# Gathers of the attention pass and the gated pass: each lot of four waits for the landing of the lot before

## The reference

```python
h_prime = (x @ W + b).reshape(n, K, F_OUT)
e = leaky_relu(h_src[src] + h_trg[trg]); e = e - max(e)
exp_e = exp(e)
alpha = exp_e / (segment_sum(exp_e, trg)[trg] + 1e-10)
out = segment_sum(h_prime[src] * alpha[:, :, None], trg)
```

```python
ei = concatenate([x[src], edge_attr], axis=-1)
core = maximum(ei @ W1 + b1, 0.0) @ W2 + b2
gate = sigmoid(ei @ Wg + bg)
agg = segment_sum(gate * core, dst)
```

## Time and profile before

| | |
|---|---|
| median of the runs shown | 4390.39 us |
| span of the profiled execution | 5143.9 us |
| busy: TensorE, its weight loads | 3848.2 us (75%), 2836.3 us (55%) |
| busy: VectorE, ScalarE, GpSimd | 2174.4 (42%), 1234.4 (24%), 1935.0 us (38%) |
| mean granted TensorE clock | 0.828 |
| gathers of the attention pass (line 865, 416) | 401.7 us busy, 386.7 us idle before them |
| gathers of the summation pass (line 865, 416) | 393.9 us busy, 211.3 us idle before them |
| gathers of the gated pass (line 865, 416) | 393.5 us busy, 563.7 us idle before them |

### The profile page before, as it was taken

The page is one execution under the profiler, slowest core; times in us unless marked ns, Lnnn a source line. Parts: engine busy times, 40 slices in busy tenths (PEclk is TensorE's granted clock), DMA queues, the critical chain, the costliest instruction groups (busy, mean ns, idle before and its releaser), DMA issues. The chain is left out here.

```text
span 5143.9 us, 62246 instructions
## 1 busy us (share of the span) xinstructions
PE 3848.2 (75%) x19117; PEld 2836.3 (55%) x19117; DVE 2174.4 (42%) x6089; ACT 1234.4 (24%) x3514; POOL 1935.0 (38%) x2021
## 2 busy tenths in 40 slices
PE   3877777234735555458399999996969999999597
PEld 2555555112425444357366665654538887777586
DVE  5555556600344444242300000005237777777723
ACT  3555454200100000012200000001125554444332
POOL 3455453474266666445400000001224444444053
PEclk8778888566866766668699999997579999999598
DMA  6655553000023333036454444443434444444266
GB/s 213 175 148 141 150 152 107 1 19 1 3 83 91 92 89 91 25 112 184 143 153 142 142 136 141 140 133 99 113 126 137 134 137 135 133 130 129 69 218 208
DMA packets 424073, 613.62 MB, mean 119 GB/s; under 512 B 149273, under 2 KB 287650, under 8 KB 423490
## 3 DMA queue, kind: packets, MB, share of 16 engines
q1 hardware_dynamic: 310578, 327.46, 22.2%
q0 software_dynamic: 104112, 273.76, 18.6%
q10 hardware_dynamic: 9056, 8.43, 0.5%
HBM read 517.83 MB, written 91.59 MB: 118 GB/s over the span
## 5 line engine op out<-in xcount | busy, mean ns | idle before, releaser
L2217 POOL DMA_INDIRECT stage<-t_row,f_take x168 | 162.1, 965 | 1269.7 <-POOLq L2064 1152.3
L865 POOL DMA_INDIRECT eg_rows<-t_edge,src_i x416 | 393.5, 946 | 563.7 <-DVE eg_pre L1698 422.1
L1108 PE MATMUL ps<-sum_hot,sum_rows 128*128 128x128 f32 x1664 | 330.0, 364 | 365.6 <-issue 201.5
L1372 PE MATMUL ps<-cv_cells,xn 128*128 128x384 f32 (+2 forms) x1600 | 535.7, 493 | 67.2 <-DMA cv_cells<-t_cells 67.2
L271 POOL DMA_INDIRECT t_cells<-times_seen,cell x416 | 409.8, 985 | 413.0 <-PEq L312 152.8
L865 POOL DMA_INDIRECT ag_rows<-t_att,src_i x416 | 401.7, 966 | 386.7 <-DVE ag_msg L970 264.6
L1108 PEld LDWEIGHTS ps<-sum_hot,sum_rows 128*128 128x128 f32 x1664 | 292.7, 264 | 403.0 <-issue 392.9
L865 POOL DMA_INDIRECT sum_rows<-t_row,src_i x416 | 393.9, 947 | 211.3 <-issue 116.5
L1050 PE MATMUL ps<-featT,ag_msg 128*128 128x128 f32 x1664 | 370.7, 357 | 127.2 <-issue 124.4
L1372 PEld LDWEIGHTS ps<-cv_cells,xn 128*128 128x128 f32 x1600 | 304.2, 190 | 279.5 <-DMA cv_cells<-t_cells 67.6
L1650 PE MATMUL ps<-eg_w,eg_rT 128*128 128x256 f32 x1664 | 439.3, 386 | 1.1 <-ACT eg_rT L1668 1.1
(11 more groups left out here) (418 smaller groups left out, 6296.4 us busy)
## 6 DMA issues: line engine op xcount, KB each, us to landing
cv_cells<-t_cells SPq DMA_DIRECT2D x225, 384.0 KB
cv_cells<-t_cells SPq DMA_DIRECT2D x75, 448.0 KB
xn<-in_L_ffn_W SPq DMA_DIRECT2D x57, 512.0 KB
t_cells<-zeros SPq DMA_DIRECT2D x17, 1664.0 KB
xn<-in_L_ffn_expert_w SPq DMA_DIRECT2D x110, 256.0 KB
ag_trow<-t_dst SPq DMA_DIRECT2D x104, 256.0 KB
t_cells<-zeros POOLq DMA_DIRECT2D x8, 1664.0 KB
eg_eaT<-in_edge_attr SPq DMA_DIRECT2D x208, 64.0 KB
```

The costliest lines, as they stand in the source:

```text
L865: nc.gpsimd.indirect_dma_start(out=rows[:, j, :], out_offset=None, in_=table, in_offset=bass.IndirectOffsetOnAxis(ap=src_i[:, n:n + 1], ax ...
L1108: mm = nc.tensor.matmul(ps[:, j % BANKS, k * EC:(k + 1) * EC], lhs, hot[:, j, :], start=True, stop=True)
L1372: mm = nc.tensor.matmul(ps[:, bank(q, k, half), 0:at.stop - at.start], source(l)[:, s, k * 128:(k + 1) * 128], cells[:, n % CR, at], start ...
L2217: nc.gpsimd.indirect_dma_start(out=xd[:, j, :], out_offset=None, in_=t_row, in_offset=bass.IndirectOffsetOnAxis(ap=take_row[:, n:n + 1], a ...
```

## The change

`gathers` gets a parameter `landed`. Where it is set, GpSimd waits ahead of each lot but the first until all four gathers of the preceding lot have landed, by the semaphores of their slots. It is set in the attention pass and in the gated pass, and not in the summation pass.

```diff
-    def gathers(pool, table, rows, ring, free, beside=None):
+    def gathers(pool, table, rows, ring, free, beside=None, landed=False):
 
         for n in range(NCH):
             j = n % ring
             if n >= ring and n % ER == 0:
                 pool.wait_ge(free.sem, free.at(n - ring + ER))
+            if landed and n > 0 and n % ER == 0:
+                for k in range(n - ER, n):
+                    pool.wait_ge(gath[k % ring].sem, gath[k % ring].at(16 * (k // ring + 1)))
             nc.gpsimd.indirect_dma_start(out=rows[:, j, :], out_offset=None, in_=table,
...
-                    gathers(pool, t_att, rows, R, g.msg_done)
+                    gathers(pool, t_att, rows, R, g.msg_done, landed=True)
...
-                    gathers(pool, t_edge, rows, GE, g.gpre_done, beside=offset)
+                    gathers(pool, t_edge, rows, GE, g.gpre_done, beside=offset, landed=True)
```

## The result

| | median, us | range |
|---|---|---|
| before | 4390.77 | 4388.14 to 4394.56 |
| changed kernel | 4773.99 | 4765.45 to 4804.88 |

The ratio is 1.0884, 95% interval 1.0853 to 1.0915: 383 us slower. Forecast were +160 (4550) and a range that ended at 4620. The direction was right, the size less than half of what came.

A forecast was written before the change was run, and what follows sets the result against it. GpSimd's issue was taken to bound the attention pass at 5.0 to 5.4 us a lot, closely followed by TensorE. Attention +160 (between +142 and +183) and gated 0 gave 4390.39 + 160 = 4550 us, range 4385 to 4620.

The forecast's parts named there:

- A lot then costs 3 x 1.25 + 2.93: Attention pass: three gather issues plus the last one's landing, 6.68 us a lot, 6.78 with the semaphores.
- The 2.93: Attention pass: us from the last gather's issue to VectorE's release, read at the opening.
- restart (four semaphores): Attention pass: four more semaphore instructions a lot, put at 0.1 us, bounds 0 and 0.30.
- The upper bound of the landing, 3.81: Attention pass: a 256 KB load of target numbers at the opening took 3.81 us; lot 7.56, +264 us.
- the gated pass's "0 us": Gated pass: new waits are met before GpSimd's existing wait for VectorE, TensorE being the bound, so no cost.
- The cover of 1.5 us: Gated pass: with a 3.81 us landing the new waits are met 1.5 us before the old wait for VectorE.
- the 753.5 us: Whole kernel: profiled span of 5143.9 us over the 4390.39 median, 17%, read as the recorder holding TensorE back.
- a span near 5072: Profiled execution: shorter rows of gathers end the stalls, attention lot from 7.48 to about 6.8 us, -72 us.
- rival A: TensorE's delays behind long gather rows are the chip's, so timed runs get faster: 72 us at most, 4328; chance 0.12.
- B: Attention pass held by something else, such as SP's loads, at 6.5 to 6.8 us a lot: no difference, 4390; chance 0.11.
- C: Attention pass: the 0.30 us between gathers is the recorder's, lot 5.8 us, +93, 4483; chance 0.20.
- The case that was left out: Attention pass: TensorE, pausing more, gets half its clock and bounds the lot at 8.2 us, some +330.

The follow-up runs named there:

- e4_sum: Kernel before with the landing wait in the summation pass alone; 5308.91 us, ratio 1.0302 (before 5153.42).
- e11_eight: Kernel before with the wait in the attention pass alone, at every second lot for the two lots before; 4577.81 us, ratio 1.0431.
- e13_numbers_once: Kernel before with the wait in the attention pass alone and target numbers loaded only for the first six lots; 5140.0 us, ratio 1.0086.
- e12_scatters: Kernel before, no wait, without the 135 scatters beside two of the experts; 4389.11 us, ratio 0.9999.
- e1_again: The kernel before, unchanged, run again; 5152.22 us, ratio 0.9994.
- e7_att: Kernel before with the landing wait in the attention pass alone; 5190.28 us, ratio 1.0183 (before 5099.84).
- e6_again: The changed kernel run again, against the kernel before at 5099.84; 5195.35 us, ratio 1.0196.
- e14_scores_once: Kernel before with the wait in the attention pass alone and blocks of target scores loaded only for the first six lots; 5244.68 us, ratio 1.0294.
- e5_lag: Changed kernel, but both passes wait for the lot before the preceding one; 5104.92 us, ratio 1.0012 to the kernel before.
- e9_one: Changed kernel, but both passes wait only for the preceding lot's last gather; 4750.84 us, ratio 1.0819 to the kernel before.
- e16_sum: Kernel before with the landing wait in the summation pass alone, a repeat; 5263.57 us, ratio 1.0334 (before 5095.6).
- e18_gated: Kernel before with the landing wait in the gated pass alone; 4420.19 us, ratio 1.0049 (before 4391.98).

## Why the prediction was wrong

**Right: the mechanism in the attention pass.** The gathers stand in fours, each row followed by a stop that the gathers' own landing ends, VectorE's long waits are gone, the six lots of the ring absorb nothing, and the pass runs at 4 gathers of issue plus landing. It is the step "A lot then costs 3 x 1.25 + 2.93", with its form borne out by e4_sum and e11_eight. Also right was that undisturbed the pass before is bound by GpSimd's issue: 5.0 to 5.4 us a lot were taken, 5.09 was found.

**Wrong: two terms of that sum.** This is the step that failed.

| term, us a lot | put | measured |
|---|---|---|
| issue of four | 3.75 + 0.95 = 4.70 | 4.85 |
| landing behind the last issue | 2.93 - 0.95 = 1.98 | 2.88 |
| restart (four semaphores) | 0.1 | 0.77 |
| lot | 6.78 | 8.50 |
| lot before | about 5.23 (160 / 103) | 5.09 |
| difference | 1.55 | 3.41 |

The landing is short by 0.90 and the restart by 0.67; with 0.15 of issue and 0.14 of the lot before, 1.86 us a lot or 192 us. The 2.93 was read on one transfer at the opening. Between the end of its issue and VectorE's start the DMA share was 0.32, against 0.54 later in the same pass:

```profile
105.90:107.80 1.90, 0.39 (x2) 0.28 (x2) 0.00 (x0) 1.85 (x6) 1.29 (x2) 0.50 0.32 84
200.00:892.00 692.00, 546.13 (x2984) 377.91 (x2983) 379.13 (x1158) 348.61 (x1003) 343.95 (x356) 0.82 0.54 144
```

In the steady pass the gather shares the DMA engines with the target numbers, which e13_numbers_once shows to cost 0.5 us; what the other 0.4 are is not shown. The upper bound of the landing, 3.81, is near the measured 0.95 + 2.88 = 3.83. It was the time of another load at the opening, so that agreement may be luck, and its lot of 7.56 is still 0.94 short, most of it the restart. The restart was given no end of its own: "bounds are 0 and the 0.30 us that stand between two gathers" were those of one more instruction, but the term is not an instruction; it is the time from a landing to the next indirect DMA. No row of before shows that for GpSimd. Its restart behind VectorE in the gated pass is short: in e12_scatters VectorE's `eg_pre` ends at 3606.22 + 0.68 = 3606.90 and GpSimd starts 0.27 us later.

```profile
3606.22 0.68 DVE L1698 TENSOR_TENSOR eg_pre<-ps,eg_rows 128x512 f32<-128x512 f32 x1
```

```profile
3607.17 0.94 POOL L865 DMA_INDIRECT eg_rows<-t_edge,src_i  x1 [3.64 <-DVE eg_pre L1698]
```

The page of the Trainium skill that I weighed there, DMA: Bandwidth & Descriptors, section Anatomy of one DMA, gives a GpSimd DMA a fixed 2.0 us and bytes over 436 GB/s. By that the landing is an estimated 2.3 us; behind the end of the issue the runs show 1.8 us (summation pass) to 2.88 in the mean. The sum in that section has no term for the restart.

**Wrong by about 32 us: the gated pass's "0 us".** The cover of 1.5 us was the difference of a wait of 4.37 us and a landing of 3.81 from the last gather's start. The landing was about right, but the cover had no restart in it, and the wait was one cycle of a slow execution. At a 4390 place the wait is 366.0 / 102 = 3.59 us, as TensorE's round is 8.38 us and not 9.05. In the changed kernel GpSimd stands still for 390.0 / 103 = 3.79 us ahead of a lot:

```profile
  POOL eg_rows L868: 390.0, 103
```

That is 0.77 of restart and 3.02 of landing. 3.59 against 3.79 is no cover at all. At 5100 places, where the prediction's rows come from, the round is longer (8.9 us in e1_again, (4763.6 - 3838.7) / 103.75, and 8.7 in e7_att), and there the 0 us held three times.

**Wrong: the reading of the 753.5 us.** "I read this as the recorder holding TensorE back" was to explain 753.5 us between recording and timing. That is refuted by e1_again (timed at 5152 without a change) and by the changed kernel's stage of 395 matmuls beside the same scatters. Every one of the 19 profiled executions was timed, and each time the span was 1.7 to 1.8 us less. The argument "something has to fill 753.5 us" did not ask whether the profiled execution was itself one of 5146 us. The Trainium skill, Runtime: NRT & Kernel Launch, section The launch sequence, whose rule I set aside as wrong by two orders, says that a profile's total is some 6 us longer than the reported time, whatever the kernel. Here the span is 1.7 us shorter than the time, so size and sign are others, but that the two differ by a few us only is what the runs show, and the 753.5 us were no evidence against it. The forecast "a span near 5072" for the profiled execution is wrong with it: the span is 4767.2 where the median is 4774, above before's 4390, and at a 5100 place (5183.4 in e6_again) it is above before's 5100 too. It cost the forecast of the time little, since the undisturbed lot it led me to was right; it gave rival A its price, and it hid the gated pass's true round.

**The rivals.** A (faster) took the stalls for the chip's. At 5100 places they are in the times, as it said, but the lot without them is longer than the stalled one, so nothing was gained there either. B (something else at 6.5 to 6.8 us a lot) was not so: undisturbed the lot is 5.09. C took the 0.30 us between gathers as the recorder's; they stand in all traces and in a lot of 5.09 = 4 x 1.27, in executions that took 1.7 us more than their span. The case that was left out, TensorE bound at half its clock, did not come either: it is 77% busy (688.11 of 894.00 us, clock 0.74) and GpSimd's chain closes without it.

**What stays open.** What delays TensorE behind long unbroken rows of indirect DMAs at some places and not at others. The two runs meant for it met 4390 places both times. Also why e14_scores_once was slower, what makes the landing vary from 1.9 to 3.6 us, and why GpSimd takes 0.7 us more to start where the landing's wait is an instruction of its own.

No version here beats the kernel before. e5_lag, which puts a bound on how far the gathers run ahead, neither cost nor brought anything clear of noise at its 5100 place (ratio 1.0012, from 1.0000).

## What to carry to other kernels

A wait on an indirect DMA's own landing in the program that issues them turns a pipelined queue into a serial one: where issue is the bound, its price is landing plus restart, once per wait, less the 0.30 us that stand between two gathers anyway. The lot can be written down before running, as 4.7 + 1.8 + 0.8 = 7.3 us for the summation pass was (7.28 and 7.47 measured). Take the landing from the middle of the pass with its traffic, not from the opening, and give the restart a term of its own; it was 0.26 us where the gather itself waited for the landing and 0.74 to 0.77 where a wait instruction ahead of it did. Before a trace is used, ask how long that very execution took; where its span and the timed runs differ by 17%, read every period and every cover as one of another execution, and state the sum for both.

## What the runs showed of the hardware

- GpSimd's next indirect DMA starts 0.77 us after the last record of a landing where waits for all four landings stand ahead of it, 0.74 where one stands ahead of it (e9_one), and 0.26 where it waits for the landing itself (six lots of e9_one). VectorE starts 0.12 us after the same record. After a semaphore of VectorE that it waits for itself, it starts in 0.27 us.
- An indirect DMA of 132 KB landed 2.88 us after the end of its issue beside the loads of the attention pass, in the mean and at a 4390 place; 2.67 at a 5100 place, and 2.15 there without the 256 KB of target numbers for each lot. The 128 KB one of the summation pass took 1.79 us in e4_sum and about 2.0 in e16_sum.
- One kernel took 4390 us at some places and 5096 to 5153 at others. In 114 us beside 91 indirect DMAs TensorE issued 29 and 60 matmuls in the profiles of the kernel before at the latter, and 391 and 395 in those of e18_gated and the changed kernel at the former.
- The span is 1.7 to 1.8 us less than the time of the same execution, in all 19.
